# Way back of the first FFN as three bf16 products, with the outputs split by ScalarE and Pool, on one Trainium2 core

## What is computed

```python
scores = jnp.einsum('ntd,ed->nte', x, gate_w)
probs = jax.nn.softmax(scores, axis=-1)
g, m = jax.lax.top_k(probs.transpose(0, 2, 1), k)   # k = 128 of 512 tokens per expert
xin = x[batch_idx, m]
h = jax.nn.gelu(jnp.einsum('nekd,edf->nekf', xin, w1), approximate=False)
h = jnp.einsum('nekf,efd->nekd', h, w2)
out_tok = g[..., None] * h
out = jnp.zeros((n, t, d), dtype=x.dtype).at[batch_idx, m].add(out_tok)
```

## Time and profile before

| | us |
|---|---|
| median of 3 runs | 2167.16 (2164.66 to 2167.8) |
| the profiled execution's own time | 2159.97 |
| its span | 2158.2 |
| PE busy | 1880.6 (87%) |
| DVE busy | 1308.8 (61%) |
| POOL busy | 819.5 (38%) |
| ACT busy | 690.8 (32%) |
| mean granted TensorE clock | 0.961 of full speed |

### The profile page before, as it was taken

How to read it: one execution, slowest core, us unless ns; L and a number is a source line. 1 busy time by engine, 2 the same in 40 slices (tenths; PEclk the granted TensorE clock), 3 DMA queues, 4 the chain that set the end, 5 groups by cost and what they waited for, 6 DMA issues and landing times.

```text
span 2158.2 us, 74372 instructions
## 1 busy us (share of the span) xinstructions
PE 1880.6 (87%) x33712; PEld 1393.5 (65%) x33712; DVE 1308.8 (61%) x2442; ACT 690.8 (32%) x1041; POOL 819.5 (38%) x747
## 2 busy tenths in 40 slices
PE   6899999999988899879999889898887988888894
PEld 4667777777766676657652466675666766667783
DVE  3867777777788778767326545565555556454224
ACT  2333333333323333324310133333332433334341
POOL 2555555555555555230103123132342313113442
PEclk9999999999999999999999999998988989989997
DMA  9400000000000000030002231221313213014566
GB/s 304 149 1 2 2 2 2 2 2 2 2 2 2 2 2 1 2 99 1 1 3 41 36 80 38 68 72 32 81 35 74 63 41 78 26 52 129 178 205 188
DMA packets 81035, 113.33 MB, mean 53 GB/s; under 512 B 9485, under 2 KB 63505, under 8 KB 80288
## 3 DMA queue, kind: packets, MB, share of 16 engines
q1 hardware_dynamic: 71376, 97.16, 16.8%
q0 software_dynamic: 4544, 8.54, 1.1%
q10 hardware_dynamic: 4800, 2.89, 0.5%
HBM read 83.25 MB, written 45.68 MB: 60 GB/s over the span
## 4 chain that ended last, share of the span: by engine, by line
PE 47%; DVE 13%; issue 6%; DMA 2%; ACT 2%; another core or an unknown queue 1%; POOL 1%; SPq 0%; POOLq 0%; DVEq 0%; ACTq 0%
PE psum L1096 45%; DVE colmax L1990 2%; DVE colmax L1821 1%; DMA arena<-in_pack 1%; DVE rowmax L1998 1%; PE psum L1443 1%; DVE ctx_sum L1849 1%; ACT arena L1577 1%; DVE arena L1794 1%; DVE raw L1809 1%; PE psum L1171 1%; DVE stats L1781 0%; DVE arena L1835 0%; PE psum L1163 0%
## 5 line engine op out<-in xcount | busy, mean ns | idle before, releaser
L1096 PE MATMUL psum<-arena 128*32 128x32 f32 (+8 forms) x10680 | 747.7, 255 | 79.8 <-issue 51.8
L1096 PEld LDWEIGHTS psum<-arena 128*32 128x32 f32 (+3 forms) x10680 | 547.7, 127 | 205.1 <-issue 123.5
L1577 ACT ACTIVATE arena<-psum 128x1024 f32<-128x1024 f32 (+1 forms) x192 | 169.5, 883 | 354.0 <-PE psum L1096 281.8
L1821 DVE TENSOR_REDUCE colmax<-psum 128x512 bf16<-128x2048 f32 (+2 forms) x96 | 168.3, 1753 | 118.4 <-PE psum L1096 118.4
L1990 DVE TENSOR_REDUCE colmax<-psum 128x256 bf16<-128x768 f32 (+2 forms) x160 | 178.4, 1115 | 89.5 <-PE psum L1096 61.0
L1096 PE MATMUL psum<-neg_ident,rowmax 128*32 128x128 bf16 (+2 forms) x4864 | 215.7, 241 | 9.6 <-issue 8.2
L1592 ACT COPY ctx_sum<-psum 128x384 f32<-128x384 f32 x128 | 61.3, 479 | 498.5 <-PE psum L1096 498.5
L1998 DVE TENSOR_REDUCE rowmax<-psum 128x2 bf16<-128x256 f32 (+1 forms) x192 | 98.1, 511 | 177.3 <-PE psum L1096 166.6
L2237 POOL TENSOR_TENSOR arena<-ctx_sum 128x256 f32<-128x256 f32 x128 | 109.0, 852 | 248.9 <-DVE ctx_sum L1849 237.6
L1096 PE MATMUL psum<-prob,ffw 128*32 128x128 f32 x5120 | 168.4, 277 | 26.4 <-DVE rowmax L1827 26.3
L1096 PEld LDWEIGHTS psum<-prob,ffw 128*32 128x32 f32 x5120 | 133.6, 110 | 82.0 <-DVE rowmax L1827 56.4
(11 more groups left out here) (269 smaller groups left out, 2709.9 us busy)
## 6 DMA issues: line engine op xcount, KB each, us to landing
arena<-in_pack SPq DMA_DIRECT2D x39, 578.0 KB
sent<-in_empty SPq DMA_DIRECT2D x9, 2112.0 KB, 35.2
arena<-qk_parts SPq DMA_DIRECT2D x96, 128.0 KB
q_copies<-arena SPq DMA_DIRECT2D x32, 256.0 KB, 3.9
prob<-q_copies SPq DMA_DIRECT2D x128, 64.0 KB, 3.6
qk_parts<-arena SPq DMA_DIRECT2D x16, 384.0 KB, 3.8
arena<-sent SPq DMA_DIRECT2D x39, 132.0 KB
ffw<-in_L_w SPq DMA_DIRECT2D x1, 2048.0 KB, 10.3
```

The lines of the kernel that those rows point to most:

```text
L1096: return pe.matmul(o, lhsT, rhs, start=start, stop=stop, skip_group_check=True)
L1577: act.activation(probs_of(i)[:, :, h0 * P:(h0 + nh) * P], slot(n)[:, 0:(i + 1) * W].rearrange("p (j c) -> p j c", c=W), ACT.Exp, scale=HD1 ...
L1821: dve.tensor_reduce(colmax[:, n % 2, :], scores_of(u).rearrange("p j c -> p c j"), AX.X, ALU.max).then_inc(colmax_dve, 1)
```

## The change

After each expert the output no longer goes into `xin` but into one of two f32 buffers `y_whole` (in `ctx_sum`), and a new step `y_split(r)` behind `down0(r)` makes three bf16 parts of it: ScalarE casts (waits `y_done`), Pool subtracts, ScalarE casts the rest (waits Pool), Pool subtracts into the third part. Parts 0 and 1 take the place of `xin` for that expert, part 2 goes to `y_low` at the start of the arena. VectorE's output of expert r waits for the split of expert r - 2. `back` becomes three bf16 products and `back`'s one-hot buffers become bf16. As `y_low` lies where the key stacks lay, `k_st` and `q_st` change places, the query stacks wait for all `back` products (`backed`), and the keys are prepared behind batch 1 and the queries behind batch 2, with `keys_out(0)` behind batch 3.

```diff
-        back = arena[:, back_at:back_at + BACKS * S].rearrange("p (a s) -> p a s", a=BACKS)
+        back = arena[:, back_at:back_at + BACKS * S // 2].bitcast(BF16).rearrange("p (a s) -> p a s", a=BACKS)
...
+        y_whole = [ctx_sum[:, z, 0, :] for z in range(2)]
+        y_low = arena[:, 0:E * B * CAP // 2].bitcast(BF16).rearrange("p (h x s) -> p h x s", h=2, x=E)
...
-        k_st = carve([H1 * S // 2], restart=True).bitcast(BF16).rearrange("p (h s) -> p h s", h=H1)
-        q_st = carve([H1 * S // 2]).bitcast(BF16).rearrange("p (h s) -> p h s", h=H1)
+        q_st = carve([H1 * S // 2], restart=True).bitcast(BF16).rearrange("p (h s) -> p h s", h=H1)
+        k_st = carve([H1 * S // 2]).bitcast(BF16).rearrange("p (h s) -> p h s", h=H1)
...
+        def y_part(hb, x, c):
+
+            if c == 2:
+                a = y_low[:, hb, x, :]
+            else:
+                a = xin[:, x, 4 * hb:4 * hb + 4, :].rearrange("p b s -> p (b s)").bitcast(BF16)[:, c * S:(c + 1) * S]
+            return a.rearrange("p (b d) -> p b d", d=D)
...
             add("down0", r=r)
+            split_y(r)
...
-        ahead = [(tokens_a, stat_a), (center_a,), (norm_a, key_a), (query_a,), (), (), (), ()]
+        ahead = [(tokens_a, stat_a), (center_a, norm_a, key_a), (query_a,), (), (), (), (), ()]
...
-            if b == 2:
+            if b == 3:
                 keys_out(0)
...
                         if b < 2:
                             w.wait_ge(y_done, 2 * E)
+                            if what == "query":
+                                w.wait_ge(backed, B * E)
...
-                        mm(psum[:, ko, :], xin[:, x, b, :], back[:, r % BACKS, :], start=(x == 0),
-                           stop=(x == E - 1)).then_inc(backed, 1)
+                        for c in range(3):
+                            ins = mm(psum[:, ko, :], y_part(hb, x, c)[:, b % HALF, :], back[:, r % BACKS, :],
+                                     start=(x + c == 0), stop=(x == E - 1 and c == 2))
+                        ins.then_inc(backed, 1)
...
+                    elif k == "y_split":
+                        r = s["r"]
+                        hb, x = divmod(r, E)
+                        for c in range(2):
+                            if c:
+                                w.wait_ge(pool_done, s.pool - 1)
+                            else:
+                                w.wait_ge(y_done, r + 1)
+                            act.copy(y_part(hb, x, c), y_whole[r % 2].rearrange("p (b d) -> p b d", d=D)).then_inc(
+                                y_cast, 1)
...
-                        dve.tensor_tensor(xin[:, x, 4 * hb:4 * hb + 4, :],
+                        if r >= 2:
+                            w.wait_ge(pool_done, y_split[r - 2].pool)
+                        dve.tensor_tensor(y_whole[r % 2].rearrange("p (s d) -> p s d", s=4),
...
+                        w.wait_ge(y_cast, 2 * r + 1)
+                        chain.mark(pool.tensor_tensor(whole, whole, y_part(hb, x, 0), ALU.subtract))
+                        chain.wait()
+                        w.wait_ge(y_cast, 2 * r + 2)
+                        chain.mark(pool.tensor_tensor(y_part(hb, x, 2), whole, y_part(hb, x, 1), ALU.subtract))
```

More of the change, by code:

```diff
@@ L662, in build, with split_y @@
         slots_transposed = choose.pop()
+        y_split = {}
+        def split_y(r):
+            y_split[r] = add("y_split", pool=2, r=r)
         add("up0", r=0)
@@ L910, in build @@
         POOL_KINDS = ("constant_parts", "stat", "project", "rotated", "late", "split_prob", "before_gather",
-                      "v_constants", "q_zero")
+                      "v_constants", "q_zero", "y_split")
         d_ident, d_c, d_wmod, d_x0, d_x, d_w0, d_wo, d_ff0, d_w1, d_iota, d_router, d_fill, d_table2 = (
@@ L960, in build @@
                                    "gate_done"))
-        up_full, hid_done, down_full, y_done, slots_full, back_ready, backed, x1_ready = (
-            semaphore(n) for n in ("up_full", "hid_done", "down_full", "y_done", "slots_full", "back_ready", "backed",
+        up_full, hid_done, down_full, y_done, y_cast, slots_full, back_ready, backed, x1_ready = (
+            semaphore(n) for n in ("up_full", "hid_done", "down_full", "y_done", "y_cast", "slots_full", "back_ready", "backed",
                                    "x1_ready"))
@@ L1425, in _ @@
                         r, ko = b * E + x, 4 + b % 2
+                        hb = b // HALF
                         w.wait_ge(y_done, 2 * E)
+                        w.wait_ge(pool_done, y_split[hb * E + x].pool)
                         w.wait_ge(x1_ready, b - 1)
                         w.wait_ge(back_ready, r + 1)
-                        mm(psum[:, ko, :], xin[:, x, b, :], back[:, r % BACKS, :], start=(x == 0),
-                           stop=(x == E - 1)).then_inc(backed, 1)
+                        for c in range(3):
+                            ins = mm(psum[:, ko, :], y_part(hb, x, c)[:, b % HALF, :], back[:, r % BACKS, :],
+                                     start=(x + c == 0), stop=(x == E - 1 and c == 2))
+                        ins.then_inc(backed, 1)
                     elif k == "value1":
@@ L2261, in _ @@
                         chain.mark(pool.tensor_tensor(parts[z][:, 2, :], tok, parts[z][:, 1, :], ALU.subtract))
+                    elif k == "y_split":
+                        r = s["r"]
+                        hb, x = divmod(r, E)
+                        whole = y_whole[r % 2].rearrange("p (b d) -> p b d", d=D)
+                        chain.wait()
+                        w.wait_ge(y_cast, 2 * r + 1)
+                        chain.mark(pool.tensor_tensor(whole, whole, y_part(hb, x, 0), ALU.subtract))
+                        chain.wait()
+                        w.wait_ge(y_cast, 2 * r + 2)
+                        chain.mark(pool.tensor_tensor(y_part(hb, x, 2), whole, y_part(hb, x, 1), ALU.subtract))
                     elif k == "v_constants":
```

## The result

The changed kernel takes 2177.35 us (median of 5 runs, 2171.1 to 2181.18), the kernel before on the same chip 2167.78 (2164.66 to 2170.24): a ratio of 1.0043, 95% interval 1.0022 to 1.0063. It is slower by 0.4%. The forecast was 2166.7 within 2157 to 2177 and no change; the result lies just outside. The profiled execution has a span of 2169.3 us, 11.1 more than before.

The account below looks back on a forecast made before the run. TensorE was taken to bound the way back; way back -20.9, experts +7.4 and second attention's start +13.0 summed to -0.5 us, giving 2166.7 us against the 2167.16 median, range 2157 to 2177.

Parts of the forecast that it names:

- A step becomes four of them, 0.86 us: Way back: one placement and three `back` products at 0.216 us each replace a step of 1.37 us.
- the -31.7 of the sum: Way back: saving in us from 61 shorter steps (30.9) and the last three (0.8), before stands and clock.
- the 0.216 of the gathers: Gathers: time in us of a bf16 product over 512 columns, used to price the way back's step.
- the last rival: Way back: changing between 32 and 128 weight rows leaves 0.1 us bare per step, +6, 2173 us; chance 0.04.
- -0.5: Whole kernel: predicted net change in us, from way back -20.9, experts +7.4 and start of second attention +13.0.
- +5.3: Way back: us charged for longer TensorE stands (+3.2) and transposes waiting for x update and centring (+2.1).
- +5.5: Way back: us charged for lower clock after stands, 4 behind batch 1 and 1.5 behind batch 2; bounds 0 and 8.
- my 2.8: Way back: predicted TensorE stand in us behind the key projection, 1.20 before the change.
- About +1.4: Experts: us charged because the gather of batch 5 waits behind the split of expert 7.
- the third rival: Experts: slower turns between ScalarE and Pool make them cost about 14 instead of 7.4, +6, 2173 us; chance 0.17.
- +13.0: Second attention's start: us lost as query stacks wait for all 64 `back` products; bounds 10.5 and 14.5.
- The 0.235 and 0.114 us: Clock reading: times taken per product after a 3.75 us stand and for same-shaped products in the experts.

Follow-up runs that it names:

- experiment 4: Changed kernel with the placement product padded by 96 rows of zeros to 128 rows: ratio 0.9999 to the kernel before, 2164.65 us.
- experiment 8: Kernel before the change with the placement product on 128 rows and nothing else: ratio 0.9906 to the kernel before, 2071.02 us.
- experiment 1: Changed kernel with second-half third parts in dead columns of `w1`, so query stacks wait only for first-half `back` products: ratio 0.9992, 2162.26 us.
- experiments 1 to 4: Four separate edits of the changed kernel: query stacks freed early 0.9992, splits moved behind gathers 1.0034, placement products in pairs 1.0046, placement on 128 rows 0.9999.
- experiment 9: The changed kernel, unaltered, measured again on another chip: 2100.39 us, ratio 1.0051 to the kernel before.
- late splits: Changed kernel with three `y_whole` buffers, splits of experts 5 to 7 behind the gathers, later ones two experts back: ratio 1.0034, 2172.68 us.

## Why the prediction was wrong

- *Way back, step.* The step of the prediction that failed is the term "A step becomes four of them, 0.86 us". It measured 1.07: 61 steps save 18.3 us and the last products 0.9, together 12.5 less than the -31.7 of the sum. I took the 0.216 of the gathers, where all products have 128 rows, for a stream that changes between 32 and 128, although already showed 0.32 us from a placement product to the next. I had the right mechanism as the last rival, at 4% and 0.1 us a step; it is 0.21, and 0.30 beside an f32 product (experiments 4, 8). With 128 rows the predicted 0.86 is there. Without this error the sum would have been near +12, not -0.5.
- *Way back, stands and clock.* Charged +5.3 and +5.5, together 10.8. With 19.2 us saved by the steps, -15.9 leaves +3.3. Nearly all of it is stands: 6.5 us in all, against 3.5 before. The longer step kept the cover thicker: at the keys TensorE stood 1.44 us instead of my 2.8, at the queries 1.28 instead of 2.0. With the short step (experiment 4) the stands were 3.11 and 2.01. So one error partly paid for the other. The clock came out at about nothing. The fall at the keys cost about 1.6 us, not 4, and none came at the queries. I had taken the low clock at the start as unchanged, but it was shorter, and that gave back about 1.7 (before, then after, 3.5 to 4 us into the way back in both). That part was luck: over the kernels with 32-row placement this spell lasts from 3 to 34 us.

```profile
1120.00:1124.00 4.00, 4.00 (x6) 1.10 (x5) 1.50 (x2) 0.00 (x0) 0.00 (x0) 0.50 0.00 0
```
```profile
1130.00:1134.00 4.00, 4.00 (x17) 1.19 (x16) 2.56 (x4) 0.00 (x0) 0.00 (x0) 1.00 0.00 0
```

- *Experts.* The path was right, but the walk along it was too short. It looks exact: gelus of expert 7 done at 1030.0 (forecast 1029.7), gather of batch 4 at 1035.1 as forecast. That is luck, since the changed kernel began its experts 2.25 us earlier in its trace. Counted from the first `up` product, the gelus are 2.6 us later than forecast and the gather costs 8.3 instead of 6.0. From the gelus on, the products took 5.1 us, with 5.4 forecast. What was missing is how much VectorE and Pool slow each other. The output of expert 4 came 1.15 us late, because two operations of the selection took 1.37 and 1.47 us beside the new subtracts instead of 0.47 and 1.21 (the first of them below: before, then after with its subtract). I had taken the selection as mostly free of this.

  Then the first subtract of expert 5 took 1.92 us beside a compare instead of 1.16, and the multiplication in front of the second probability cast 1.32 instead of 0.8. "About +1.4" for the gather of batch 5 measured 3.4, and 1.1 more came behind: another subtract took 2.02, and part of that gather ran at 1.2 GHz, which I had not charged. This is the third rival in kind, not in size: two subtracts of the chain passed 1.6 us, the others took 1.15 to 1.35. Its time, 2173, is among the nearest to the result and had 17%, but it kept the step of 0.86, so that nearness says little.

```profile
1008.78 0.47 DVE L1894 TENSOR_SCALAR prob<-prob 32x512 f32<-32x512 f32 x1
```
```profile
1006.53 1.37 DVE L1929 TENSOR_SCALAR prob<-prob 32x512 f32<-32x512 f32 x1
...
1006.28 1.34 POOL L2305 TENSOR_TENSOR ctx_sum<-ctx_sum,arena 128x512 f32<-128x512 f32 x1 [4.83 <-ACT arena L1666]
```

- *Second half.* Charged nothing; it cost nothing.
- *Start of attention.* +13.0, measured +12.7; right, and experiment 1 shows the cause. The six stacks need 13.8 us from issue to the first product (1206.68 to 1220.52). The about 2 us that the Trainium skill (DMA: Bandwidth & Descriptors, "Anatomy of one DMA") gives as the fixed cost of a DMA stand there for one issued by GpSimd; these were six, issued by SP, and the figure was no guide.
- *The clock at attention and the rest.* Little of the +3.8 seems to be the change's: the profiled executions of experiments 1 to 4, all with its splits, take 943.7 to 945.2 there, 0.2 to 1.7 more than before. The -2.25 at the start is of the same kind: nothing was changed in that stretch, and over all profiled executions it takes 970.2 to 978.9 us.
- *A slip in the working.* The 0.235 and 0.114 us that the prediction compares for the clock are per recorded entry, two to an f32 product, not per product. Their ratio, and with it the reading of the clock, is right.

By stretches, -0.5 became +11.1, by 12.5 for the step, 5.4 for the experts and 1.5 of untouched parts, less 7.5 for stands and clock and 0.3 at the seam.

## What to carry over

A product's price in one stream need not hold in another: look at the spacing of starts where products of different row counts alternate, and pad the small operand to the large one's rows if nothing else changes. When storage is moved, ask which transfer now waits for its last reader, and whether dead columns elsewhere serve as well. Work that is done by two engines in turns has the length of the whole chain, not of its busy times; put it where neither engine feeds a waiting stage.

## What the hardware showed that I had not expected

- The change between 32 and 128 rows cost 0.21 us per step of two changes with bf16 products and 0.30 with f32 (1.07 and 1.37 us against 0.86 and 1.07). Only 32 and 128 rows were tried.
- VectorE's compare of 128x1024 and a Pool subtract delay one another by most of an operation. The twelve last compares of the gathers, minimum, median and maximum in ns, before, after, and with late splits:

```profile
L1930 DVE TENSOR_TENSOR arena<-arena,posT x12: 1209/1218/2208, 1029.9 to 1047.3; 128x1024 bf16<-128x1024 f32 x12
```
```profile
L1965 DVE TENSOR_TENSOR arena<-arena,posT x12: 1212/2168/2177, 1035.9 to 1057.8; 128x1024 bf16<-128x1024 f32 x12
```
```profile
L1969 DVE TENSOR_TENSOR arena<-arena,posT x12: 1212/1219/2202, 1032.8 to 1050.1; 128x1024 bf16<-128x1024 f32 x12
```

  The minimum is 1.21, the slow ones take 2.17, 0.96 more, where a Pool subtract alone takes 1.15. Pool's subtracts took 1.3 to 2.02 among them. The Trainium skill (GPSIMD Engine Reference, "Key points") has them contend where VectorE reads two SBUF inputs, as here; the trace agrees, and the price is most of the Pool operation.
- Chips differ: with the same program, the changed kernel, it is 947.3 us from the first band product to the end on one and 875.2 on another (experiment 9). The granted clock in the window 1400 to 1600 us, of the kernel before and, on another chip, of the kernel before with 128 rows (experiment 8):

```profile
1400.00:1600.00 200.00, 174.20 (x5816) 131.62 (x5816) 112.04 (x279) 68.93 (x96) 59.88 (x62) 0.93 0.23 55
```
```profile
1400.00:1600.00 200.00, 179.68 (x6295) 140.42 (x6288) 122.44 (x307) 73.22 (x101) 64.16 (x68) 0.97 0.30 70
```

  The mean clock is 4% higher, while the stretch is 8% shorter, so the clock seems to explain a part only. Why is open, and whether it is the chip or the time of the run was not separated.
